# A Mamba block and a ternary feed-forward on one Trainium2 core: the D u term moved from VectorE into TensorE's fold, and the gate moved from GpSimd to VectorE

## The reference

```
x, z   = split(hidden @ in_proj.T)                  # 512 channels each
u      = silu(causal_conv4(x) + conv_b)
dt, B, C = split(u @ x_proj.T)                      # 64, 16, 16
delta  = softplus(dt @ dt_proj.T + dt_b)
h      = exp(delta * A) * h + (delta * u) * B       # over 2048 steps, 512 channels x 16 states
y      = sum_n(h * C) + u * D
y      = y * silu(z)
x1     = layernorm(hidden + y @ out_proj.T)
out    = layernorm(x1 + ffn(x1))                    # silu(W1) * W2, two hidden gelu layers, W3
```

## Time and profile before

| | us |
|---|---|
| three runs: lowest, median, highest | 3101.23, 3103.60, 3104.07 |
| the profiled execution, its own time | 3103.29 |
| its span, from the first to the last instruction | 3101.5 |
| VectorE busy | 2338.7 (75%) |
| TensorE busy | 2724.2 (88%) |
| ScalarE busy | 2010.8 (65%) |
| GpSimd busy | 1784.3 (58%) |
| mean granted TensorE clock | 0.918 |

### The profile page before, as it was taken

How to read it: one execution, slowest core, us unless ns; L and a number is a source line. 1 busy time by engine, 2 the same in 40 slices (tenths; PEclk the granted TensorE clock), 3 DMA queues, 4 the chain that set the end, 5 groups by cost and what they waited for, 6 DMA issues and landing times. The chain is left out here.

```text
span 3101.5 us, 39954 instructions
## 1 busy us (share of the span) xinstructions
PE 2724.2 (88%) x11028; PEld 1636.8 (53%) x11028; DVE 2338.7 (75%) x2781; ACT 2010.8 (65%) x3383; POOL 1784.3 (58%) x920
## 2 busy tenths in 40 slices
PE   5788988888888888888888876889999999999997
PEld 2243443343343333333333332678888888888886
DVE  5999999999999999999999999434444454444442
ACT  3777777777777777777777777555555445555442
POOL 3899999899899899999999999400000000000000
PEclk8888898989889889889889887899999999999999
DMA  7366466466475475564565566542222222222210
GB/s 254 93 189 166 121 192 163 117 190 164 118 194 149 131 197 134 145 195 127 155 183 130 164 166 192 199 159 87 83 68 88 74 68 87 89 68 83 80 41 15
DMA packets 239642, 411.98 MB, mean 133 GB/s; under 512 B 23264, under 2 KB 63456, under 8 KB 239456
## 3 DMA queue, kind: packets, MB, share of 16 engines
q1 hardware_dynamic: 175680, 297.67, 35.3%
q10 hardware_dynamic: 63776, 112.22, 11.2%
HBM read 285.55 MB, written 124.26 MB: 132 GB/s over the span
## 5 line engine op out<-in xcount | busy, mean ns | idle before, releaser
L1267 DVE TENSOR_TENSOR_SCAN h<-bank,state,db 128x512 f32<-128x512 f32 x1024 | 1252.5, 1266 | 70.9 <-ACT bank L908 37.5
L1118 POOL TENSOR_TENSOR hc<-h,c_rows 128x1024 f32<-128x1024 f32 x512 | 1202.0, 2378 | 15.3 <-DVE h L1267 10.4
L908 ACT ACTIVATE bank<-d_bc,a_neg 128x512 f32<-128x512 f32 x1024 | 692.8, 685 | 314.5 <-DVE h L1267 201.9
L1627 ACT ACTIVATE hring<-s_bank,sc 128x512 f32<-128x512 f32 x248 | 170.5, 688 | 488.9 <-PE s_bank L1560 488.5
L1560 PE MATMUL s_bank<-mid,h_r 128*128 128x512 f32 x2048 | 469.1, 390 | 4.6 <-DVEq L1654 4.6
L722 PE MATMUL bank<-x_t,w 128*128 128x512 f32 x1088 | 394.1, 492 | 55.8 <-ACT ab L972 46.9
L1251 DVE TENSOR_TENSOR db<-bank,du_bc 128x2048 f32<-128x2048 f32 x192 | 435.1, 2266 | 8.1 <-issue 7.8
L1560 PEld LDWEIGHTS s_bank<-mid,h_r 128*128 128x128 f32 x2048 | 385.8, 188 | 85.6 <-ACTq L1598 5.0
L1129 POOL TENSOR_TENSOR db<-du_bc,b_row 128x2048 f32<-128x2048 f32 x64 | 291.7, 4558 | 102.4 <-DVE h L1267 97.7
L629 PE MATMUL bank<-bc,w_spread 64*128 64x512 f32 x272 | 155.6, 581 | 217.7 <-DVE db L1251 214.5
L650 PE MATMUL bank<-hc,fold_w 128*32 128x512 f32 x2048 | 334.6, 731 | 8.6 <-DVE u L1291 5.0
(11 more groups left out here) (143 smaller groups left out, 3698.1 us busy)
## 6 DMA issues: line engine op xcount, KB each, us to landing
ab<-ab ACTq DMA_DIRECT2D x272, 256.0 KB, 4.1
du_bc<-du_rows SPq DMA_DIRECT2D x256, 256.0 KB, 4.9
d_bc<-d_rows SPq DMA_DIRECT2D x256, 256.0 KB, 7.9
s_abr<-ab SPq DMA_DIRECT2D x120, 512.0 KB, 3.9
w<-w ACTq DMA_DIRECT2D x136, 256.0 KB, 3.9
d_rows<-sp_r SPq DMA_DIRECT2D x64, 256.0 KB, 2.0
du_rows<-sp_w SPq DMA_DIRECT2D x64, 256.0 KB, 2.0
x<-res SPq DMA_DIRECT2D x17, 512.0 KB, 8.9
```

Source lines behind the costliest of these rows:

```text
L908: act.activation(decays[DECAY_BANK[g]][:], d_bc[c % 2][:, j, :], ACT.Exp, scale=a_neg[:, g:g + 1]).then_inc(decay, 1)
L1118: pool.tensor_tensor(hc[:, k % HCSTEPS, at:at + HG], h[:, H_SLOT[k], at:at + HG], c_rows[:, q, :].unsqueeze(1).broadcast_to([P, HG, NT]), ...
L1267: dve.tensor_tensor_scan(h[:, H_SLOT[k], j, :], decays[DECAY_BANK[g]][:], db[:, k % DBSTEPS, j, :], state[:, g:g + 1], ALU.mult, ALU.add). ...
L1627: act.activation(hring[c % RING][:], p_h[m % HBANKS][:], ACT.Gelu, scale=sc[:, 2 + layer, m:m + 1]).then_inc(gelu, 1)
```

## The change

TensorE adds D u itself: for each block, four matmuls of 32x32 (a diagonal block of D each, `w_skip`) with u as moving operand add into the same partitions of p_y as the fold's four, ahead of the fold in step q = 3, 2, 1 and 1 of blocks 0 to 3. Each takes 32 partitions of rows and 32 of columns, at (32 j, 32 j). VectorE then does the gate at the slot where skip was, reading p_y and z: it gives the product to `gated`, on which also the next block's first fold waits. GpSimd has no gate any more. `w_skip` is made from the fold's matrix and D before the first tile by four operations on VectorE; D arrives in a part of db, by the same number of DMAs as before. Some small tensors share a place, so that w_skip finds room.

```
-SKIP_AFTER, GATE_AFTER = GC - JC + FOLD_AFTER + 1, GC - JC + FOLD_AFTER + 3
+GATE_AFTER = GC - JC + FOLD_AFTER + 1
+SKIP_STEP = (3, 2, 1, 1)
...
+        w_skip = sb("w_skip", [P, KI, GD])
...
-                (dpar[:], D_param),
+                (db[:, 1, 0, P:P + KI], D_param),
...
             def fold_step(t, k):
                 c, q = divmod(k, QN)
                 if q == 0:
-                    pe.wait_ge(y_sb, t.count(KI, c + 1))
+                    pe.wait_ge(gated, t.count(KI, c + GATED0))
+                if q == SKIP_STEP[c]:
+
+                    for j in range(JC):
+                        at = slice(GD * j, GD * j + GD)
+                        pe.matmul(p_y[at, :], w_skip[at, c, :], u_of(t, c)[at, :], start=False, stop=False,
+                                  tile_position=(GD * j, GD * j))
                 pe.wait_ge(hc_done, t.count(TURNS * NK, TURNS * (k + 1) + HC0))
...
-            def gate(t, c):
-                pool.wait_ge(y_sb, t.count(KI, c + 1 + 1))
-                pool.wait_ge(silu_z, t.count(1, 1))
-                pool.tensor_tensor(z_of(t, c), u_of(t, c), z_of(t, c), ALU.mult).then_inc(gated, 1)
...
             for j in range(KI):
+                dve.tensor_scalar(w_skip[:, j, :], fold_w[:], db[:, 1, 0, P + j:P + j + 1], None, ALU.mult)
...
-            def skip(t, c):
-                u = u_of(t, c)
+            def gate(t, c):
                 dve.wait_ge(folded, t.count(NK, QN * (c + 1) + FOLDED0))
-                dve.scalar_tensor_tensor(out=u, in0=u, scalar=dpar[:, c:c + 1], in1=p_y[:],
-                                         op0=ALU.mult, op1=ALU.add).then_inc(y_sb, 1)
+                dve.wait_ge(silu_z, t.count(1, 1))
+                dve.tensor_tensor(z_of(t, c), p_y[:], z_of(t, c), ALU.mult).then_inc(gated, 1)
```

More of the change, by code:

```diff
@@ L243, in mamba_stage @@
         fold_w = sb("fold_w", [P, GD])
+        w_skip = sb("w_skip", [P, KI, GD])
         taps = sb("taps", [P, KI, TAPS])
-        cb = sb("cb", [P, KI])
-        dtb = sb("dtb", [P, KI])
-        dpar = sb("dpar", [P, KI])
+        cb_dtb = sb("cb_dtb", [P, 2 * KI])
+        cb, dtb = cb_dtb[:, 0:KI], cb_dtb[:, KI:2 * KI]
         a_neg = sb("a_neg", [P, NG])
@@ L252, in mamba_stage @@
         mv = sb("mv", [P, SUB, 2])
-        var4, y4, a4, nb4 = (sb(name, [P, SUB]) for name in ("var4", "y4", "a4", "nb4"))
+        var4, y4 = (sb(name, [P, SUB]) for name in ("var4", "y4"))
+        a4_nb4 = sb("a4_nb4", [P, 2 * SUB])
+        a4, nb4 = a4_nb4[:, 0:SUB], a4_nb4[:, SUB:2 * SUB]
         eps_col = sb("eps_col", [P, 1])
@@ L315, in mamba_stage @@
         folded = sem("folded")
-        y_sb, gated = sem("y_sb"), sem("gated")
+        gated = sem("gated")
         ln_dve, ln_act, ln_pool, ln_out = sem("ln_dve"), sem("ln_act"), sem("ln_pool"), sem("ln_out")
@@ L1107, in _ @@
             pool.sem_inc(db_pool, POOL0)
-            pool.sem_inc(gated, GATED0)
             def times_c(t, k):
@@ L1190, in tile @@
                         norm(t)
[L1191 to L1194, removed]
             def round_piece(j):
@@ L1242, in _ @@
             dve.sem_inc(db_dve, DVE0)
-            dve.sem_inc(y_sb, 1)
+            dve.sem_inc(gated, GATED0)
             def times_b(t, k):
@@ L1370, in tile @@
                         low_rows(nxt)
-                    if n % GC == SKIP_AFTER % GC:
-                        now, g = at_group(t, n - SKIP_AFTER)
+                    if n % GC == GATE_AFTER % GC:
+                        now, g = at_group(t, n - GATE_AFTER)
                         if exists(now):
-                            skip(now, g // GC)
+                            gate(now, g // GC)
                     if t is LAST_ROW[-1]:
```

## The result

The changed kernel takes 3084.0 us (median of 4 runs, 3080.2 to 3090.8) against 3103.8 us of the kernel before on the same chip: a ratio of 0.994, with a 95% interval of 0.9922 to 0.9958. The profiled execution took 3080.23 us, with a span of 3078.4 us.

A forecast was written before the change was run, and what follows sets the result against it. VectorE, busy 95.5% of the Mamba stage, was taken as the bound, with only its waits recoverable. Terms -1 - 1.5 + 5 = +2.5 us gave 3106 us; forecast 3099 to 3114 us (0.45), range 3088 to 3130 us.

The forecast's parts named there:

- GpSimd's relief: GpSimd loses the gate, 83 us busy; at most 3 us can return through the chain before scan 60; taken as -1 us.
- the wait before scan 60: VectorE's wait for GpSimd in each tile, about 1.8 us, 18.5 us in 1200; forecast to remain after the change.
- VectorE's gate: The gate replacing skip on VectorE: 0.68 us instead of 0.739, 3.8 us in all; taken as -1.5 us, ends 0 and -4.
- The price of the groups: TensorE's four added matmuls per block run at once like a fold step: 1.0 us at full clock, 1.9 us cold.
- rival (d): The four blocks do not run at once on TensorE, 3.6 us warm and 7.2 cold: 3168 us, chance 0.09.
- Step 13: Block 3's group: 1.3 us reaches VectorE's gate in half of the tiles, 10 us, half recovered through ScalarE: +5 us.
- the wait of 0.58 us: TensorE's wait at 1022.30 before step 13 in one tile, taken to cover 0.6 of the group's 1.9 us.
- The gate's wait: VectorE's wait for the fold ahead of block 3's gate, forecast to grow from 4.3 to some 10 us in 1200.
- The later products: TensorE's products that ScalarE copies after the added groups: taken as 0, between +16 (1 us a tile) and -13 us.
- Rival (a): TensorE's clock comes up as waits before steps 9 and 13 shrink, worth 13 us: 3088 us, chance 0.20.
- the wait of 4.50 us: TensorE's wait before step 6, longer than what step 3 adds; the argument that the clock would not come up.
- 47.5 us of waits: VectorE's waits for ScalarE, GpSimd and the fold in 1200 us, called all that relieving other engines can return.

The follow-up runs named there:

- e3: The changed kernel with GpSimd's old load given back as a useless product of u and z at the old gate's place: 3085.8 us, ratio 0.9953.
- e2: The changed kernel without the added matmuls, D u missing from the output: 3091.5 us, ratio 0.9964 to the kernel before.
- e5: The changed kernel without the added matmuls, but with GpSimd's old load given back: 3102.3 us, ratio 1.0001 to the kernel before.
- e11: The changed kernel with block 3's group ahead of the fold of step 15 instead of step 13: 3125.5 us, ratio 1.0066 to the kernel before.
- e9: The kernel before with zero-weight matmuls for block 3 alone (step 13), four a tile: 3085.0 us, ratio 0.994.
- e10: The kernel before with zero-weight matmuls for blocks 1 and 2 alone (steps 6 and 9): 3111.2 us, ratio 1.0017.
- e4: The kernel before with zero-weight matmuls for block 0 alone (step 3): 3107.0 us, ratio 1.002.
- e7: The kernel before with zero-weight matmuls for blocks 1 to 3, without block 0's group: 3084.7 us, ratio 0.9953.
- e1: The kernel before with all 16 added matmuls a tile at the change's places, weights zero, skip and gate as before: 3085.6 us, ratio 0.995.
- e6: The kernel before with zero-weight groups only ahead of the two long db waits, three before the 4.50 us one, two before the 3.60 us one: 3107.3 us, ratio 1.0019.
- e12: The changed kernel with zero-weight groups ahead of the two long db waits and one more before each wait ahead of steps 13 and 14: 3067.4 us, ratio 0.9886.
- e8: The changed kernel with zero-weight groups ahead of the two long db waits, as in e6: 3074.4 us, ratio 0.9919 to the kernel before.

## Why the prediction was wrong

**GpSimd's relief, -1 us.** Right for the changed kernel: e3 gave the load back and nothing changed that the runs can tell, and the wait before scan 60 stayed (18.5 us before, 18.4 us after). But without the matmuls the same relief is worth 10 us (e2 against e5), more than the 3 us that the prediction gave as its bound from the one large wait. So the -1 is in part luck, and the way of the 10 us is open.

**VectorE's gate, -1.5 us.** 0.676 us against 0.739, a saving of 0.06 as forecast. In e5 it is worth nothing that can be told, but the interval there reaches 3 us to each side, so -1.5 is neither shown nor excluded.

**The price of the groups.** Right: 0.99 us from start to start at full clock (1045.78 to 1046.77 in e11's timeline), 1.86 us at the low clock, as a fold step. Four row blocks ran at once on one bank: in the changed kernel's trace the four matmuls of a group start within 20 ns. The rule under "Gotcha 1: PSUM Pressure" of the Trainium skill's page TensorEngine Tiling (Array Packing), by which different row tiles cannot use the same PSUM bank at one time, does not hold for the time here, where each block has its own 32 partitions, and rival (d) is out.

**Step 13, +5 us.** This is the step that failed. It took 1.9 us for the group, subtracted the wait of 0.58 us and carried the other 1.3 us to the gate of block 3, with the clock of everything behind it unchanged. In fact the group took the place of idle time in the wait for db, and the clock came up before step 14: the fold there is shorter by 0.87 us, and the products behind it run at the full clock too. In the tiles shown, 11.3 us lie between the folds of steps 13 and 15 instead of 14.9, of which only 0.6 were the wait; in the mean of twelve tiles it is 12.3 instead of 15.2, and only 0.6 of the 2.9 us between them is idle time. The gate's wait went from 4.3 us to 0.2 instead of to 10. TensorE is then earlier over the whole tile boundary (the folds of steps 15, 0 and 1 by 1.3 to 1.4 us against their scans), ScalarE waits less for its products (50.2 us instead of 64.8), and the decays before scans 10 and 12 are in time in more of the tiles. The order of these three is read from the traces; no run separates them. e9 shows that this place gives the whole gain by itself, e11 that with the group at step 15 the change costs 20 us.

**The later products, 0 between +16 and -13.** Both signs were there, at different places. By themselves the groups at steps 6 and 9 cost about 5 us (e10), the one at step 3 about 5 us (e4), and that at step 13 gives 20 us (e9). With step 13 in place the others cost nothing that these runs can tell (e9 0.994, e7 0.9953, e1 0.995).

**Rival (a)** came true in sign and nearly in size, 3088 forecast, 3084 measured, and had a chance of 0.20. The size is in part luck: its 13 us were a third of the waits for decays, taken without a reason for a third (they fell from 24.7 to 13.7 us in the 1200), and it had nothing for the gate's wait for the fold, which fell by 4.1 us there. Its place was half wrong: it named the waits before steps 9 and 13 alike, while e6 shows that the full clock around steps 6 and 9 gains nothing in the kernel before, and e10 that groups at these steps cost something. Its argument against, that the wait of 4.50 us stays, was true (the fold of step 6 is at the low clock in every middle tile after the change) and did not matter. What pointed to step 13 was in the trace of the kernel before: a stretch from the fold of step 13 to that of step 15 with a clock of 0.69 and 15.4 of 16.0 us busy. Another sign there misleads. The six tiles in which the fold of step 5 was at the low clock are just those in which VectorE waited 1.5 us before scan 35, yet e9 has the whole gain with that wait in four tiles.

**A smaller slip.** The 47.5 us of waits that the prediction calls all that any relief can return leave out 4.0 us at line 1274, where VectorE waits for ScalarE; no term of the sum rests on it.

## What to carry to other kernels

A price of an added matmul that is taken with the clock held fixed can have the wrong sign: before it is summed, look for the places where the low clock covers work with no wait behind it that could take it up, and ask whether the added work fills the idle time just ahead of them. There a few matmuls that add zero are worth trying by themselves, place by place, since their effect is read off in one run each: here the changed kernel was 20 us faster than the one before with the group at step 13, and 20 us slower with the same group two steps later. The mean clock of a stage doesn't tell which of these places it is.

## What was not expected of the hardware

- Seven groups a tile that add zero took the changed kernel from 3084.0 to 3067.4 us (e12), while TensorE is not the engine with the highest share in the stage (1550 of 1800 us busy in the changed kernel, VectorE 1733).
- The same zero-weight groups in the same waits made the kernel before 0.2% slower (e6) and the changed kernel 0.2 to 0.3% faster (e8).
- The mean granted clock of the stage was 0.89 in a kernel that gained 20 us (e9) and 0.91 in one that lost 5 (e6).
- Four 32x32 float32 matmuls of 512 columns on the diagonal of the array, writing 32 partitions each of one bank in the midst of another accumulation group, take 0.99 us together at full clock, as long as four of 128x32.
